# A macaron transformer layer on eight cores: four blocks instead of two transposed by TensorE in the first stage, W1 in two halves, one more first cycle taken into that stage, and statistics from two instructions instead of four

## The chip, the cores and the metric

One Trainium2 chip, eight cores, one sequence (4096 tokens by 1024 features) on each; the cores run the same program and exchange nothing. The metric is the device time of the slowest core in microseconds (us).

## The reference

For each sequence, with `ln` a layer norm without weights:

```
x = x + 0.5 * ffn(ln(x));  x = x + attention(ln(x));  x = x + 0.5 * ffn(ln(x))

ffn(x):  gf = sigmoid(small net of the mean of x over all tokens)
  three times:  tf = sigmoid(gelu(gelu(gelu(out@w1+b1)@w2+b2)@w3+b3)@w4+b4)    # one number a token
                c = 0.1 + adaptive_range * (0.7*gf + 0.3*tf - 0.5) * 2
                out = out + c * [p_r, -p_i, -o_r, o_i]        # quarters o_r o_i p_r p_i of out
```

The attention is causal and linear, with a memory term; it takes no part in the change. The mean over the tokens has to be known before the first coupling `c`, so nothing past the first call of the coupling net can start before every token is normalised.

## The kernel before

The tokens go in 8 blocks of 512, each of 4 tiles of 128. Every engine has its program written out by hand, and the tables at the head of the file set which piece stands where; nothing is moved by a scheduler. There are four stages: P (normalise all tokens), A (first ffn), B (attention), C (second ffn). The change is in P and at the start of A.

**Stage P** runs over the tiles i = 0 to 31. SP's queue loads tile i into a ring of 8 (`x0_ring`), DVE takes its statistics (four `bn_stats` over 256 features and one `bn_aggr`), GpSimd makes scale and bias of a pair of tiles, ACT writes the normalised tile as bf16 (`xtok`, `xtok_b`) three iterations later, TensorE adds the tokens up (`token_sums`, one matmul column for each 128 features and tile). SP waits for the normalised tile i-8 before it loads tile i, since that frees its place in the ring. Blocks 0 and 1 are transposed by TensorE (`transposes`, then copied to `xt` by ACT and DVE). Blocks 2 to 7 are stored to HBM and come back through DMA transposes (`load_xt`), two of which, for blocks 2 and 3, stand in SP's queue ahead of the loads of tiles 24 and 28.

**The UV groups.** W1 is applied once for each block: 24 groups of four matmuls, in threes. K (`xs` times W1, `xs` a sum of features) is copied by ACT to `kt`; U and V are joined with `kt` by DVE to the tiles `u` and `v`. DVE prepares `w1n` and changes two parts of `w1` first (`prepare_w1`), four instructions over 2048 elements.

**A cycle** (block b, k = 0, 1, 2) is the coupling net: ACT makes `h1` by gelu in four parts (`gelu1`), TensorE runs layer 2 (32 matmuls), ACT gelus its four banks (`gelu2`), layer 3 (8 matmuls), `gelu3`, layer 4 (2), `tanh4`. From the tanh DVE makes `c` and the next `p1` (`coupled`), ACT the next `h1`. UV groups of a later block stand as fillers in three places of each cycle: behind layer 2, behind layer 3, behind layer 4 (`FILL`). Cycle 0 of block 0 stands within stage P (`P_L2`, `P_L3`, `P_L4`: the iterations of its layers), since it needs no `c`. In each block of A, ACT also forms the new x of the block before (`spread`, four instructions for each tile), DVE adds it (`combine`), and ACT normalises it for stage B.

**PSUM.** All 8 banks go round in the order in which TensorE takes them (`Banks`): a group waits until the bank taken eight places earlier is read out. K's bank is freed by ACT's copy, U's and V's by DVE.

Of the kernel before, what the change touches and what calls it, by code (L numbers as in the profile page):

```python
# [38 lines left out]
FILL_FIRST = [(0, 0, 0), (2, 2, 5), (2, 3, 0)]  # L39
# [11 lines left out]
P_UV = {**{4 + i: (0, i) for i in range(8)}, **{12 + i: (1, i) for i in range(5)},  # L51
        18: (1, 5), 19: (1, 6), 20: (1, 7), 24: (2, 0), 25: (2, 1)}
P_L2, P_L3, P_L4 = 17, 19, 20
P_SUMS = {4 * b + 7: b for b in range(2, NB - 1)}
P_LAST = 10
# [15 lines left out]

def fillers(ph, b, k, place):
# [3 lines left out]
    if ph == "A" and b == 0:  # L76
        items += [("UV", ahead, g) for g in part(FILL_FIRST, k, place, P_LAST)]
    elif ahead is not None:
        items += [("UV", ahead, g) for g in part(FILL, k, place)]
# [57 lines left out]
def emit(plan, final):  # L137
# [56 lines left out]
    v_x, _ = sb("v_x", [128, DT, T], BF16, xa3 + 8192)  # L194
    gw1c, _ = sb("gw1c", [128, DT, 512], BF16, xa + 16384)
# [62 lines left out]
    bnq, _ = sb("bnq", [128, 2, NTT, 4, 6], F32)  # L258
# [9 lines left out]
    qsum, _ = sb("qsum", [128, NTT, 4], F32)  # L268
# [36 lines left out]
    w1_ld = sig("w1_ld")  # L305
# [46 lines left out]

    def xt_item(ph, b):
        return "ABC".index(ph) * NB + b
# [20 lines left out]
    def tensor_program(te):  # L375
# [21 lines left out]
        def xt_ready(ph, b):  # L397
            if ph == "A" and b < 2:
                te.wait_ge(*freed_at(("T", "P", b, 1)))
                te.wait_ge(*freed_at(("T", "P", b, 3)))  # L400
            else:
                te.wait_ge(*xt_ld[b % 2].at((ph, b)))

        def uv_group(ph, b, g):
# [3 lines left out]
            if g == 0:  # L408
                xt_ready(ph, b)
                te.wait_ge(*xs_ok.at((ph, b)))  # L410
                te.wait_ge(*w1n_ok.at(ph))
            bk = take(("UV", ph, b, g))
            for n in range(4):
                if which == 0:
                    lhs, rhs = w1[:, K_TILES[n], cols], ffn[ph]["xs"][:, n, :]
# [278 lines left out]
    def scalar_program(s):  # L694
        def normalize(ph, b, tt):
# [30 lines left out]
        def transposed(b):  # L726

            for bk2 in range(2):
                bk, use = banks.at(("T", "P", b, bk2))
                s.wait_ge(bank_full[bk], use + 1)  # L730
                s.activation(out=pair(xt[:, b], bk2),
# [58 lines left out]
        def tanh4(ph, b, k):  # L790
            if b > 0 and k == 0:
# [3 lines left out]
            s.activation(out=ffn[ph]["th"][:, k, :], in_=ps[:, bk, :], func=AF.Tanh, scale=0.5,  # L795
# [42 lines left out]
        def cycle(ph, b, k):  # L838
            if k > 0:
# [3 lines left out]
            if b > 0 and k == 1:  # L843
# [3 lines left out]
            if b > 0 and k == 2 and ph == "A":  # L847
                normalize("A", b - 1, 1)
            if ph == "A" and b > 1 and k == 0:
                normalize("A", b - 2, 3)  # L850
            gelu2(ph, b, k)
            filler(ph, b, k, 0)
            if k == 2 and b + 1 < NB:
                for p in range(3):
                    gelu1(ph, b + 1, 0, p)
            gelu3(ph, b, k)
            filler(ph, b, k, 1)
            if k == 2 and b + 1 < NB:
                gelu1(ph, b + 1, 0, 3)
            tanh4(ph, b, k)  # L860
            if b > 0 and k < 2:
                spread(ph, b - 1, 2 * k)
            if b > 0 and k == 2:
# [29 lines left out]
        for i in range(4, 32):  # L893
            if i >= 7:
                normalize("P", (i - 3) // 4, (i - 3) % 4)
            if i == P_L3:
                gelu3("A", 0, 0)
            if i == P_L4:
                s.wait_ge(*misc_ok.at("misc"))
                tanh4("A", 0, 0)  # L900
            if i in P_UV:
                k_group("A", P_UV[i][0], 3 * P_UV[i][1])
            if i == 10:
                transposed(1)
# [12 lines left out]
        for b in range(NB):
            for k in range(3):
                if b > 0 or k > 0:
# [51 lines left out]
    def vector_program(v):  # L971
# [5 lines left out]
        def statistics(ph, b, tt):  # L977
# [10 lines left out]
            for q in range(4):  # L988
                i = v.bn_stats(out=bnq[:, b % 2, tt, q, :], in_=src[:, q * 256:(q + 1) * 256])
# [4 lines left out]
        def transposed(b):  # L994

            for bk2 in range(2, 4):
                bk, use = banks.at(("T", "P", b, bk2))
                v.wait_ge(bank_full[bk], use + 1)
                v.tensor_copy(out=pair(xt[:, b], bk2),
# [20 lines left out]
        def feature_sums(ph, b):  # L1020

            if ph == "A" and b < 2:
# [4 lines left out]
            if b > 0:  # L1027
# [3 lines left out]
            x, xs = xt[:, b % 2], ffn[ph]["xs"]  # L1031
# [4 lines left out]
        def prepare_w1(ph):  # L1036

            w1n = ffn[ph]["w1n"]
            if ph == "C":
                v.wait_ge(*freed_at(("QK", "q", NB - 1, DT - 1)))  # L1040
                v.scalar_tensor_tensor(out=w1n[:, 0:2, :], in0=w1[:, 0:2, :], scalar=2.0,
                                       in1=w1[:, 4:6, :], op0=ALU.mult, op1=ALU.add)
                v.scalar_tensor_tensor(out=w1n[:, 2:4, :], in0=w1[:, 6:8, :], scalar=2.0,
                                       in1=w1[:, 2:4, :], op0=ALU.mult,
                                       op1=ALU.add).then_inc(*w1n_ok.up(ph))
                return
            v.wait_ge(*w1_ld.at("w1"))
# [671 lines left out]
```

## Time and profile before

| what | us |
|---|---|
| median of 3 runs (1725.27 to 1735.0) | 1725.83 |
| the profiled execution, device time | 1724.32 |
| its span, slowest core (6); all cores 1715.6 to 1722.8 | 1722.8 |
| PE busy in the span | 1594.4 (93%) |
| DVE, ACT busy | 1004.0, 894.1 |
| first layer 2 that needs `c` (block 0, cycle 1) starts | 145.74 |
| cycle 0 of block 2 starts | 230.37 |

The span counts from the first to the last instruction of the core. A start time in a row is in us from the span's start.

### The profile page before, as it was taken

What the parts mean: (1) busy time and instruction counts of PE and PEld (TensorE: products, weight loads), DVE (VectorE), ACT (ScalarE), POOL (GpSimd) and SP (SyncE); (2) the same over time, 40 slices, a digit from 0 to 9 for tenths busy, and PEclk for the clock granted to TensorE, in tenths of its full rate; (3) what the DMA queues carried; (4) which work ended last, traced back from release to release, by engine and by line L of the source; (5) the groups of instructions that cost most, each with busy time, mean ns of one, the idle gap of its engine ahead of it and who ended that gap; (6) DMA issues with size and microseconds to landing.
All of it is one profiled execution on the core that took longest, in us unless ns stands there. A gap on an engine that the chain in (4) does not pass through costs nothing.

```text
span 1722.8 us, 27449 instructions; the slowest of 8 cores (1715.6 to 1722.8 us)
## 1 busy us (share of the span) xinstructions
PE 1594.4 (93%) x8166; PEld 726.6 (42%) x8166; DVE 1004.0 (58%) x1856; ACT 894.1 (52%) x1350; POOL 303.6 (18%) x873
## 2 busy tenths in 40 slices
PE   3947999999998999999999999999999999999973
PEld 1423444444443444444444444444444444444431
DVE  4865665565465574536364554545465566767653
ACT  2554787776678714050413233241525677777774
POOL 2541232122023220101101020202020011011111
PEclk9978999999999999999999999999999999999996
DMA  8897124563175983132415142332331123332223
GB/s 196 193 292 163 56 84 124 142 159 105 55 157 131 218 223 90 71 104 68 129 37 159 25 147 50 123 74 86 92 123 25 25 97 101 121 116 81 98 98 122
DMA packets 171422, 196.56 MB, mean 114 GB/s; under 512 B 125328, under 2 KB 132496, under 8 KB 170000
## 3 DMA queue, kind: packets, MB, share of 16 engines
q1 hardware_dynamic: 149024, 111.18, 24.5%
q0 software_dynamic: 22256, 83.64, 16.6%
q8 instruction: 71, 1.16, 0.3%
q14 instruction: 71, 0.58, 0.1%
HBM read 100.16 MB, written 80.74 MB: 105 GB/s over the span
## 4 chain that ended last, share of the span: by engine, by line
PE 83%; ACT 5%; DVE 5%; issue 3%; DMA 2%; SPq 2%; POOL 0%; DVEq 0%; ACTq 0%; POOLq 0%
PE ps L431 20%; PE ps L514 13%; PE ps L420 12%; PE ps L566 7%; PE ps L503 6%; PE ps L579 6%; PE ps L594 6%; PE ps L442 5%; PE ps L489 3%; PE ps L538 2%; PE ps L583 2%; DMA x_ring<-hs 1%; ACT h_a L773 1%; SPq L1598 1%; ACT h_c L773 1%
## 5 line engine op out<-in xcount | busy, mean ns | idle before, releaser
L723 ACT ACTIVATE xtok<-xr,st_nmr,st_r 128x1024 bf16<-128x1024 f32 x32 | 39.7, 1240 | 312.5 <-POOL st_nmr L1408 312.5
L431 PE MATMUL ps<-h_a,w 128*128 128x512 bf16 x768 | 176.0, 387 | 17.6 <-ACT h_a L773 16.8
L431 PE MATMUL ps<-h_c,w 128*128 128x512 bf16 x768 | 175.9, 386 | 16.7 <-ACT h_c L773 16.6
L874 ACT ACTIVATE ebuf<-ps 128x512 bf16<-128x512 f32 x128 | 76.1, 595 | 130.9 <-PE ps L514 127.6
L420 PE MATMUL ps<-xt,w 128*128 128x512 bf16 x512 | 135.0, 387 | 0.0
L431 PEld LDWEIGHTS ps<-h_a,w 128*128 128x128 bf16 x768 | 74.1, 99 | 117.5 <-issue 36.8
L431 PEld LDWEIGHTS ps<-h_c,w 128*128 128x128 bf16 x768 | 73.9, 99 | 117.2 <-issue 37.4
L566 PE MATMUL ps<-wmo,sq 128*128 128x512 bf16 x512 | 121.3, 383 | 1.0 <-DVE xr L1256 1.0
L1364 POOL TENSOR_SCALAR tmp<-mv 128x1 f32<-128x1 f32 (+2 forms) x56 | 13.3, 238 | 602.8 <-DVE mv L991 600.9
L503 PE MATMUL ps<-wvo,xt 128*128 128x512 bf16 x512 | 113.0, 379 | 0.0
L514 PE MATMUL ps<-xt,wk_sb 128*128 128x512 bf16 x512 | 111.8, 379 | 0.0
L514 PE MATMUL ps<-xt,wq_sb 128*128 128x512 bf16 x512 | 111.8, 379 | 0.0
L579 PE MATMUL ps<-s_bf,sq 128*128 128x512 bf16 x448 | 105.8, 379 | 0.0
L1012 DVE SCALAR_TENSOR_TENSOR u_c<-ps,pack,kt_C 128x512 bf16<-128x512 f32 x64 | 47.9, 749 | 94.7 <-ACT kt_C L745 88.2
L594 PE MATMUL ps<-v_sb,skt 128*128 128x512 bf16 x448 | 97.8, 379 | 0.0
L1012 DVE SCALAR_TENSOR_TENSOR u_a<-ps,pack,kt_A 128x512 bf16<-128x512 f32 x56 | 41.8, 747 | 81.7 <-ACT kt_A L745 77.7
L1173 DVE TENSOR_SCALAR ebuf<-ebuf 128x512 bf16<-128x512 bf16 x128 | 37.2, 290 | 82.4 <-ACT ebuf L874 81.6
L780 ACT ACTIVATE h_C<-ps,pack 128x512 bf16<-128x512 f32 x96 | 58.1, 688 | 51.1 <-PE ps L431 51.1
L773 ACT ACTIVATE h_c<-p_c 128x1024 bf16<-128x1024 bf16 x64 | 65.9, 1053 | 31.0 <-DVE p_c L1102 28.4
L420 PE MATMUL ps<-xs_A,w 128*128 128x512 bf16 x256 | 68.3, 391 | 14.2 <-DVE xs_A L1033 7.8
L773 ACT ACTIVATE h_a<-p_a 128x1024 bf16<-128x1024 bf16 x64 | 65.9, 1053 | 29.4 <-DVE p_a L1102 26.3
L1261 DVE SCALAR_TENSOR_TENSOR xr<-ps,rlm,xr 128x512 f32<-128x512 f32 x64 | 48.0, 750 | 54.2 <-PE ps L583 50.3
(217 smaller groups left out, 2891.5 us busy)
## 6 DMA issues: line engine op xcount, KB each, us to landing
x_d<-xr POOLq DMA_DIRECT2D x64, 512.0 KB, 3.7
xr<-x_d SPq DMA_DIRECT2D x60, 512.0 KB, 3.6
x_ring<-hs SPq DMA_DIRECT2D x32, 512.0 KB, 8.4
xr<-hs SPq DMA_DIRECT2D x32, 512.0 KB, 4.5
xn_d<-xtok POOLq DMA_DIRECT2D x64, 256.0 KB, 3.2
out<-xr POOLq DMA_DIRECT2D x32, 512.0 KB, 3.1
sk_d<-sk SPq DMA_DIRECT2D x7, 1024.0 KB, 5.1
w<-cw POOLq DMA_DIRECT2D x6, 512.0 KB, 14.5
```

Source lines behind the costliest of these rows:

```text
L420: i = te.matmul(out=ps[:, bk, :], lhsT=lhs, rhs=rhs, start=(n == 0), stop=(n == 3))
L431: i = te.matmul(out=ps[:, bks[et], :], lhsT=w2[:, kt, et * 128:(et + 1) * 128], rhs=ffn[ph]["h1"][:, kt, :], start=(kt == 0), stop=(kt == ...
L442: i = te.matmul(out=ps[:, bks[et], :], lhsT=w3[:, kt, et * 128:(et + 1) * 128], rhs=ffn[ph]["h2"][:, kt, :], start=(kt == 0), stop=(kt == 3))
L503: i = te.matmul(out=ps[:, bk, :], lhsT=xt[:, b % 2, dt, tt * 128:(tt + 1) * 128], rhs=wvo[:, dt, eh * T:(eh + 1) * T], start=(dt == 0), st ...
L514: i = te.matmul(out=ps[:, bk, :], lhsT=w_sb[:, dt, et * 128:(et + 1) * 128], rhs=xt[:, b % 2, dt, :], start=(dt == 0), stop=(dt == DT - 1))
L566: i = te.matmul(out=ps[:, bk, :], lhsT=sq[:, dt, tt * 128:(tt + 1) * 128], rhs=wmo[:, dt, eh * T:(eh + 1) * T], start=(dt == 0), stop=(dt ...
L579: te.matmul(out=ps[:, bk, :], lhsT=sq[:, dt, tt * 128:(tt + 1) * 128], rhs=s_bf[:, dt, eh * T:(eh + 1) * T], start=(dt == 0), stop=False)
L594: i = te.matmul(out=ps[:, bk, :], lhsT=skt[:, jt, dt * 128:(dt + 1) * 128], rhs=v_sb[:, jt, eh * T:(eh + 1) * T], start=(jt == 0), stop=(j ...
L773: s.activation(out=pair(ffn[ph]["h1"], p), in_=src, func=AF.Gelu).then_inc(*h1_ok.up((ph, b, k, p)))
L780: s.activation(out=ffn[ph]["h2"][:, et, :], in_=ps[:, bk, :], func=AF.Gelu, bias=pack[:, P_B2 + et:P_B2 + et + 1]).then_inc(bank_free[bk], 1)
L874: s.activation(out=ebuf[:, n % 2, :], in_=ps[:, bk, :], func=AF.Exp).then_inc(*e_ok.up(n))
L1012: v.scalar_tensor_tensor(out=u[:, et, :], in0=ps[:, bk, :], scalar=pack[:, P_B1 + et:P_B1 + et + 1], in1=ffn[ph]["kt"][:, et % 2, :], op0= ...
```

## The change

- **Four blocks are transposed by TensorE** (`P_TURNED`, `P_T`: blocks 1, 2, 3 at i = 10, 15, 22). Blocks 0 to 3 are neither stored nor loaded back, and the two DMA transposes leave SP's queue in stage P.
- **W1 comes in two column halves**, eight loads instead of four. `prepare_w1` runs for each half (the second at i = 6). SP no longer waits for W1 before it loads tile 4. The loads of W2 and W3 are issued by GpSimd behind tile pair 4 instead of 2, those of the small net behind pair 9 instead of 6.
- **Cycle 0 of block 1 moves into stage P** (layers at i = 24, 26, 27), with its own buffers `th_1` and `xs_1`. Four thirds of block 2's UV groups stand in P instead of two, so 12 groups; with the four at the end 16 of 24. Block 1 has two cycles in stage A, which hold all 24 groups of block 3 and the spreads and normalised tiles of block 0. DVE does block 1's first `coupled` and `turn` at the end of block 0's last cycle.
- **Statistics** are two `bn_stats` over 512 elements. Their input alternates between two quarters of the features, 1024 bytes apart, so that the even and the odd half of the result are a quarter each, and GpSimd needs one instruction less for a block. This holds for stage B's statistics too.
- The load of `wv` for stage B is issued after block 1's couplings instead of after the small net.

```diff
-FILL_FIRST = [(0, 0, 0), (2, 2, 5), (2, 3, 0)]
+FILL_FIRST = [(0, 0, 3), (1, 1, 3), (0, 0, 0)]
+FILL_SECOND = [(0, 0, 0), (4, 4, 6), (5, 5, 0)]
...
+P_TURNED = 4
+P_T = {10: 1, 15: 2, 22: 3}
+P_L2 = {17: 0, 24: 1}
...
 def xt_ready(ph, b):
-            if ph == "A" and b < 2:
+            if ph == "A" and b < P_TURNED:
...
         def cycle(ph, b, k):
-            if k > 0:
+            second = (ph, b) == ("A", 1)
+            if k > first_cycle(ph, b):
                 for p in range(4):
                     gelu1(ph, b, k, p)
                 filler(ph, b, k - 1, 2)
...
             tanh4(ph, b, k)
-            if b > 0 and k < 2:
+            if second:
+                spread(ph, 0, 2 * k - 2)
+                spread(ph, 0, 2 * k - 1)
+                if k == 2:
+                    normalize("A", 0, 1)
+            elif b > 0 and k < 2:
                 spread(ph, b - 1, 2 * k)
...
         def statistics(ph, b, tt):
-            for q in range(4):
-                i = v.bn_stats(out=bnq[:, b % 2, tt, q, :], in_=src[:, q * 256:(q + 1) * 256])
+            for q in range(2):
+                i = v.bn_stats(out=bnq[:, b % 2, tt, q, :],
+                               in_=src[:, q * 512:(q + 1) * 512].rearrange("p (c j) -> p j c", c=2))
...
+        def prepare_w1(half_):
+            w1n = ffn["A"]["w1n"][:, :, half_ * 512:(half_ + 1) * 512]
+            w = w1[:, :, half_ * 512:(half_ + 1) * 512]
+            v.wait_ge(*w1_ld[half_].at("w1"))
...
         for i in range(SEQ // 128):
-            if i == 4:
-                q.wait_ge(*w1_ld.at("w1"))
-            if i == 24:
-                load_xt("A", 2)
-            if i == 28:
-                load_xt("A", 3)
...
-            if i >= 16:
+            if i - 8 >= 4 * P_TURNED:
                 store_normalized(i - 8)
```

The order on TensorE in stage P from i = 23 to i = 27, before (L525 token sums, L420 the UV groups of i = 24 and 25; nothing stands at i = 22 and 26):

```order
L525 MATMUL ps<-onesz,xtok 128x1 x32
L420 MATMUL ps<-xs_A,w_43 128x512 x4
L420 MATMUL ps<-xt,w_43 128x512 x4
L420 MATMUL ps<-xt,w1n_A 128x512 x4
L420 MATMUL ps<-xs_A,w_43 128x512 x4
L420 MATMUL ps<-xt,w_43 128x512 x4
L420 MATMUL ps<-xt,w1n_A 128x512 x4
L525 MATMUL ps<-onesz,xtok_b 128x1 x32
```

And now, from i = 22 to 26 (L415 transposes, L448 UV groups, L553 token sums, L459 layer 2, L470 layer 3):

```order
L415 MATMUL ps<-idb,xtok_b 128x128 x32
L553 MATMUL ps<-onesz,xtok_b 128x1 x32
L448 MATMUL ps<-xs_A,w_43 128x512 x4
L448 MATMUL ps<-xt,w_43 128x512 x4
L448 MATMUL ps<-xt,w1n_A 128x512 x4
L553 MATMUL ps<-onesz,xtok 128x1 x32
L459 MATMUL ps<-h_a,w_44 128x512 x32
L448 MATMUL ps<-xs_A,w_43 128x512 x4
L448 MATMUL ps<-xt,w_43 128x512 x4
L448 MATMUL ps<-xt,w1n_A 128x512 x4
L470 MATMUL ps<-h_A,w_45 128x512 x8
```

Block 3's transposes and a second layer 2, with its layer 3, have come in between the UV groups.

TensorE in cycle 2 of block 0, with the layer 2 that starts it and the one behind it, before:

```order
L431 MATMUL ps<-h_a,w_44 128x512 x32
L420 MATMUL ps<-xt,w_43 128x512 x4
L420 MATMUL ps<-xt,w1n_A 128x512 x4
L442 MATMUL ps<-h_A,w_45 128x512 x8
L420 MATMUL ps<-xs_A,w_43 128x512 x4
L420 MATMUL ps<-xt,w_43 128x512 x4
L420 MATMUL ps<-xt,w1n_A 128x512 x4
L451 MATMUL ps<-h_A,w4r 128x512 x2
L431 MATMUL ps<-h_a,w_44 128x512 x32
```

And now, with the last three groups of cycle 1 ahead (L459, L470, L479 are layers 2, 3 and 4):

```order
L448 MATMUL ps<-xs_A,w_43 128x512 x4
L448 MATMUL ps<-xt,w_43 128x512 x4
L448 MATMUL ps<-xt,w1n_A 128x512 x4
L459 MATMUL ps<-h_a,w_44 128x512 x32
L470 MATMUL ps<-h_A,w_45 128x512 x8
L479 MATMUL ps<-h_A,w4r 128x512 x2
L459 MATMUL ps<-h_a,w_44 128x512 x32
```

Between layers 2, 3 and 4 of block 0's cycle 2 nothing stands any more.

ACT in block 1 from the tanh of cycle 1 to the `gelu2` of cycle 2, before (L759 spread, L773 `gelu1`, L745 the copy of K, L723 normalise):

```order
L795 ACTIVATE th_A<-ps,misc 128x512
L759 ACTIVATE tq_a<-xr,tk 128x256 x4
L773 ACTIVATE h_a<-p_a 128x1024 x4
L745 ACTIVATE kt_A<-ps 128x512
L723 ACTIVATE xtok<-xr,tk 128x1024
L780 ACTIVATE h_A<-ps,pack 128x512 x4
```

And now, the same place (L790 spread, L804 `gelu1`, L776 the copy of K, L752 normalise):

```order
L826 ACTIVATE th_A<-ps,misc 128x512
L790 ACTIVATE tq_a<-xr,tk 128x256 x8
L804 ACTIVATE h_a<-p_a 128x1024 x4
L776 ACTIVATE kt_A<-ps 128x512 x2
L752 ACTIVATE xtok<-xr,tk 128x1024
L811 ACTIVATE h_A<-ps,pack 128x512 x4
```

Two spreads stand ahead of the four parts of `gelu1`, and the copies of K behind them.

## Rows read from the trace of the kernel before

**Rows 1.** Busy time by stretch: us, engines, then clock, DMA share, GB/s.

```profile
40.00:60.00 20.00, 20.00 (x146) 10.53 (x145) 19.07 (x47) 11.91 (x15) 8.98 (x26) 1.00 0.63 117
...
100.00:120.00 20.00, 8.77 (x59) 4.06 (x59) 13.51 (x38) 10.09 (x10) 10.10 (x29) 0.71 0.99 274
120.00:140.00 20.00, 8.64 (x116) 5.05 (x117) 7.68 (x25) 6.89 (x12) 8.76 (x30) 0.52 0.70 242
```

**Rows 2.** Chain that ended last, two issues in it: start, us, what.

```profile
90.12 8.52 SPq L1598
...
104.32 9.62 SPq L1598
```

**Rows 3.** Waits of SP's queue, 0 to 60 us: total, times, longest.

```profile
SPq L1622 <- DMA w<-cw: 20.9, 1, 20.9
```

**Rows 4.** Timeline of DVE, first stage: start, length, instruction, idle before.

```profile
29.98 1.22 DVE L1048 TENSOR_TENSOR w1n_A<-w 128x2048 bf16<-128x2048 bf16 x1
...
43.85 1.40 DVE L989 BATCH_NORM_STATS2 bnq<-x_ring 128x6 f32<-128x256 f32 x4
...
45.53 0.74 DVE L1012 SCALAR_TENSOR_TENSOR u_a<-ps,pack,kt_A 128x512 bf16<-128x512 f32 x1
...
46.79 1.40 DVE L989 BATCH_NORM_STATS2 bnq<-x_ring 128x6 f32<-128x256 f32 x4
...
58.52 1.28 DVE L999 COPY xt<-ps 128x1024 bf16<-128x1024 bf16 x2
...
89.33 0.75 DVE L1012 SCALAR_TENSOR_TENSOR u_a<-ps,pack,kt_A 128x512 bf16<-128x512 f32 x1 [5.81 <-ACT kt_A L745]
...
127.62 0.26 DVE L991 BATCH_NORM_AGGREGATE mv<-bnq 128x2 f32<-128x24 f32 x1
```

**Rows 5.** Timeline of PE, first stage and blocks 0 and 1.

```profile
78.61 7.07 PE L431 MATMUL ps<-h_a,w 128*128 128x512 bf16 x32
...
145.74 8.81 PE L431 MATMUL ps<-h_a,w 128*128 128x512 bf16 x32 [5.22 <-ACT h_a L773]
...
178.58 7.07 PE L431 MATMUL ps<-h_a,w 128*128 128x512 bf16 x32
185.49 1.03 PE L420 MATMUL ps<-xs_A,w 128*128 128x512 bf16 x4
...
187.21 1.89 PE L442 MATMUL ps<-h_A,w 128*128 128x512 bf16 x8
188.94 1.03 PE L420 MATMUL ps<-xt,w1n_A 128*128 128x512 bf16 x4
...
190.67 0.59 PE L451 MATMUL ps<-h_A,w4r 128*128 128x512 bf16 x2
191.10 1.03 PE L420 MATMUL ps<-xt,w 128*128 128x512 bf16 x4
...
230.37 7.07 PE L431 MATMUL ps<-h_a,w 128*128 128x512 bf16 x32 [0.17 <-issue]
```

**Rows 6.** Timeline of ACT, the same stretch.

```profile
85.13 2.42 ACT L780 ACTIVATE h_A<-ps,pack 128x512 bf16<-128x512 f32 x4 [5.85 <-PE ps L431]
...
88.55 0.61 ACT L745 ACTIVATE kt_A<-ps 128x512 f32<-128x512 f32 x1
...
130.24 2.37 ACT L723 ACTIVATE xtok_b<-x_ring,st_nmr,st_r 128x1024 bf16<-128x1024 f32 x2 [2.50 <-POOL st_nmr L1377]
...
173.77 2.96 ACT L773 ACTIVATE h_a<-u_a 128x1024 bf16<-128x1024 bf16 x3
...
191.99 2.06 ACT L759 ACTIVATE tq_a<-xr,tk 128x256 f32<-128x256 f32 x4
```

**Rows 7.** DVE's groups by line and shape, whole span: count, busy, mean ns.

```profile
L1080 DVE STREAM_TRANSPOSE ctr_A<-th_A 32x384 f32<-32x384 f32 x32 | 18.2, 569 | 13.2 <-ACT th_A L795 12.8
...
L1217 DVE TENSOR_TENSOR a_t<-ps,mask 128x512 bf16<-128x512 f32 x8 | 5.5, 692 | 21.8 <-PE ps L538 21.8
...
L1217 DVE TENSOR_TENSOR a_t<-ps,mask 128x256 bf16<-128x256 f32 x8 | 3.4, 424 | 2.2 <-PE ps L538 2.2
```

More of the change, by code:

```diff
@@ L76, in fillers @@
     if ph == "A" and b == 0:
-        items += [("UV", ahead, g) for g in part(FILL_FIRST, k, place, P_LAST)]
+        items += [("UV", ahead, g) for g in part(FILL_FIRST, k, place, P_LAST + 4)]
+    elif ph == "A" and b == 1:
+        items += [("UV", ahead, g) for g in part(FILL_SECOND, k, place)]
     elif ahead is not None:
@@ L304, in emit @@
     skt_ld = sig("skt_ld")
-    w1_ld = sig("w1_ld")
+    w1_ld = [sig(f"w1_ld{i}") for i in range(2)]
     w2_ld = sig("w2_ld")
@@ L842, in cycle @@
                 filler(ph, b, k - 1, 2)
-            if b > 0 and k == 1:
+            if b > 0 and k == 1 and not second:
                 spread(ph, b - 1, 1)
@@ L1077, in token_couplings @@
                 v.wait_ge(*tok_ok.at((ph, b - 1)))
-            rows = ffn[ph]["th"][:, :, :].rearrange("p k t -> p (k t)")
-            for q in range(4):
-                i = v.transpose(out=ffn[ph]["ctr"][32 * q:32 * q + 32, :, :],
-                                in_=rows[32 * q:32 * q + 32, :].rearrange(
-                                    "p (a t) -> p a t", t=128)[:, :, 32 * q:32 * q + 32])
+            k0 = first_cycle(ph, b)
+            parts = [(ffn[ph]["th"][:, k0:, :].rearrange("p k t -> p (k t)"), 4 * k0, 12)]
+            if k0 == 1:
+                parts.append((tanh_row(ph, b, 0), 0, 4))
+            for rows, first, last in parts:
+                for q in range(4):
+                    i = v.transpose(out=ffn[ph]["ctr"][32 * q:32 * q + 32, first:last, :],
+                                    in_=rows[32 * q:32 * q + 32, :].rearrange(
+                                        "p (a t) -> p a t", t=128)[:, :, 32 * q:32 * q + 32])
             i.then_inc(*ctr_ok.up((ph, b)))
@@ L1221, in attention @@
             if b == NB - 1:
[L1222 removed]
+                restore_w1n()
             bk, use = banks.at(("D", b))
@@ L1301, in vector_program @@
         feature_sums("A", 0)
-        prepare_w1("A")
+        prepare_w1(0)
         token_sums("P", 0)
@@ L1489, in gpsimd_program @@
         step(g.memset(half[:, 0:1], -0.5))
-        step(g.memset(tmp[:, :, :], 0.0))
-        g.memset(qsum[:, :, :], 0.0).then_inc(*iota_ok.up("iota"))
-        load(w1, cw1, DT, 2, w1_ld, "w1")
+        g.memset(tmp[:, :, :], 0.0).then_inc(*iota_ok.up("iota"))
+        g.wait_ge(*iota_ok.at("iota"))
+        for h in range(2):
+            c = slice(512 * h, 512 * (h + 1))
+            load(w1[:, :, c], cw1[:, :, c], DT, 2, w1_ld[h], "w1")
         for j in range(2 * NB):
```

203 lines of the change are left out of this document (117 added, 86 removed).

## The prediction

> **What bounds the kernel now.** I read the windows first, then the chain that ended last, then SP's waits, then the three timelines. PE is the bound of the whole, but not of stage P: in 100 to 140 us it is busy 17.4 of 40 us, at a granted clock of 0.71 and 0.52 [rows 1]. In 40 to 60 us DVE is busy 19.07 of 20 us [rows 1]: an iteration takes 43.85 to 46.79 = 2.94 us, of which the statistics are 1.68 (to the next instruction at 45.53) and the U and V of one third 1.26 [rows 4]. Two things break that pace. At the layer 2 of i = 17 DVE waits 5.81 us for `kt` [rows 4], because ACT's copy stands behind the four parts of `gelu2` and a normalise [rows 6]: from the start of layer 2 (78.61) to the U behind it (89.33) it is 10.7 us [rows 4, 5]. And in the chain stand the two DMA transposes, which hold SP's queue for 8.52 and 9.62 us [rows 2], so that the last tiles are asked for late. Before that SP had waited 20.9 us for W1 [rows 3].
>
> The stage ends when the last tile is normalised, 130.24 + 2.37 = 132.6 [rows 6]; the first layer 2 that needs `c` starts 13.1 us later, at 145.74, and block 2's first cycle at 230.37 [rows 5]. From there on the two programs do the same work, so the question is how far that point moves.
>
> **Stage P, before its first layer 2.** The four parts of `prepare_w1` at 2048 elements take 1.22 us each, from 29.98 on [rows 4]; a half takes four of about 0.6, and one wait, so 32.6 in place of 34.7. PE can do its first K meanwhile, and the first iteration ends at about 36.8. The statistics: the row of 512 elements against that of 256 gives 692 - 424 = 268 ns for 256 elements [rows 7], so of the 350 ns for one `bn_stats` about 70 are fixed; two of 512 take 1.2 to 1.27 us instead of 1.40, which leaves 1.55 for a tile and 2.80 for an iteration. So i = 6 starts at 39.6 (before 43.85). Then DVE pays 2.5 for the second half of W1, 1.3 for each transposed block (58.52 starts such a copy, 1.28 [rows 4]) and the sums of features as before: i = 10 ends at 56.1, i = 12 at 65.7 (PE's wait for `xs` as before), i = 15 at 74.1. PE then transposes block 2 and sums it, and layer 2 starts at 75.7 instead of 78.61.
>
> **From there to the end of stage P.** With 10.7 us from layer 2 to the next U, and 2.8 for each further iteration that has U and V, i = 18 ends at 87.7, i = 21 at 97.0, i = 23 (with block 3's transposes in between) at 102.8. The second layer 2 starts at about 101 (behind the third at i = 23 and its token sums), so U of i = 25 comes at 111.8, and DVE waits nearly 6 us again, a stall that was not there. i = 26, 27, 28 end at 116.0, 117.5 and 120.3, and three statistics later DVE is through at 125.0 (before 127.62 + 0.26 = 127.9 [rows 4]). The way from there to the normalised tile was 4.7 us (GpSimd's four instructions and ACT's two), so the stage ends at 129.7 instead of 132.6. Removing the two transposes from SP takes 18.1 us out of the chain and brings only 2.9: what is late next is DVE, held by ACT and PE at two layers 2. The loads are early enough: tile 31 can be asked for at 113, when tile 23 is normalised, and is wanted at 123.4. Two more short stretches of transposes and token sums may leave the clock low at a layer 2; I take 0.9 us for that. **Stage P: -2.0 us.** The 13.1 us behind it stay, since three groups are now done in a gap of 5.22 us on PE [rows 5].
>
> **From the first layer 2 to block 2.** Before, 230.37 - 145.74 = 84.6 us. In them lie five cycles and 38 groups. A cycle's own layers are 6.91 + 1.73 + 0.43 = 9.07 us (178.58 to 185.49, 187.21 to 188.94, 190.67 to 191.10), two groups 1.73 [rows 5]: 45.4 + 32.8 = 78.2, so 6.4 us are idle or slow. Now four cycles and 29 groups: 36.3 + 25.1 = 61.3. What is added by waits:
> - 1.7 us as before for the low clock at the first layer 2 (8.81 for 7.07 [rows 5]).
> - Block 0, cycle 1: one group behind layer 2 and one behind layer 3, for gelus of 2.42 and 1.26 us, and three behind layer 4, 2.6 us, for a way through tanh, `c`, `p1` and gelu of 4.7 us: 2.9 us.
> - Block 0, cycle 2: no group at all. Behind layer 2 ACT does `gelu2` (2.42 [rows 6]), then three parts of block 1's `gelu1` (2.96 [rows 6]), then `gelu3` (1.2). Layer 4 ends about 7.2 us behind layer 2, and PE works 2.2 of them: 5.0 us.
> - Block 1, cycle 1 to 2: ACT does two spreads (2 x 2.06 [rows 6]) ahead of the four parts of `gelu1`, and only then copies K. The fourth bank that the next layer 2 takes is that of such a K group (eight takes earlier), so it waits for tanh 0.74, spreads 4.1, gelus 4.2, copy 0.5 = 9.6 us, under which lie six groups, 5.2 us: 4.4 us.
> - The end of block 1 with two more spreads and three normalised tiles ahead of the next `gelu2`: 1.0, and 1.5 in cycle 0 of block 2, which is past the point and counts all the same.
>
> Together 16.5, so 77.8 instead of 84.6: **-6.8 us.** Bounds: if none of the new waits appears (they are worked out, not seen) it is -17; if the clock falls to the lower level in the two long ones it is some 3 us less, so -4.
>
> Edits that I cost at nothing: the later load of `wv`, since block 3's folds use it a block of some 48 us later; W2, asked for at 54 instead of 45 and wanted at 75.7, which is close, and costs one us for each us it lands later; stage B's statistics, since PE is the bound there; GpSimd's missing instructions.
>
> **Sum.** -2.0 - 6.8 = -8.8 on the profiled execution's 1724.3 (1.5 above its span) gives 1715.5; the median of the runs is 1.5 above that execution, so **1717 us**.
>
> **Rivals.**
>
> *Slower: the interleaved reads cost DVE double.* No row shows DVE reading float32 from SBUF in jumps at each element. The nearest is the 32x384 transpose, which jumps after each 32 elements and takes 569 ns, as 384 elements at 1.05 ns and a fixed part would [rows 7]; by it I take no penalty. At two element times a tile would cost 2.55 instead of 1.55. Stage P is DVE's up to layer 2: the twelve statistics ahead of it (and the work between, unchanged) put it at 87.3, behind it the two waits for `kt` hide a part, and the end comes at 145.7 + 4.7 = 150.4, 17.8 late. With -6.8 it is +11, so 1737. It decides from 0.45 us more for a tile on. The Trainium skill (Advanced Engine Details and Errata, SBUF Cachelines) states that SBUF has 16-byte cachelines, that two hits on a line are needed to absorb the access latency, and that a different line at each access is penalised; the changed input hits a line once. No row here can confirm it, and by that rule this rival is the forecast.
>
> *Faster: stage P runs at DVE's own work.* If the second stall doesn't appear and the first is shorter, DVE needs 32.7 + 28 x 1.55 + 20 x 1.26 + 10 of copies, sums and W1 = 111 for its last tile, 17 earlier than 127.9. With the rest as above it would be -24. Against it stands the row of 5.81 us, for it the loads, which come much earlier. Half of it is likelier than all: 1700 to 1706.
>
> *No change.* Tiles 4 to 7 are now asked for beside W1, and W1 in pieces of half the length. If tile 3 or W1's first half lands 4 us later, or W2 after 75.7, the -2.0 turns into +2, and with the low clock in both new waits 1724 remains. SP might also be held by something other than the transposes; then its gain is nothing, which is the same case.
>
> **Chances.** Forecast 0.45 (own range 1708 to 1725), slower rival 0.27 (1729 to 1746), faster rival 0.15, no change 0.13. The range from 1701 to 1740 leaves out about 2 in 10. Over 1% (17.3 us, about what this kernel's measurement can tell) faster is most of the faster rival and a tail of the forecast: 0.18. Slower by as much is the upper part of the slower rival: 0.09. Within 1%: 0.73.
>
> **What would show it.** One `bn_stats` of 512 at 0.6 to 0.7 us (right) or 1.1 to 1.2 (slower rival). No DMA transpose on SP before 140 us. The two layers 2 of stage P at about 76 and 101, each with DVE waiting some 5 us for `kt`. The last tile normalised near 130. Gaps on PE of 5 us in block 0's cycle 2 and 4 us ahead of block 1's second layer 2, the latter ended by ACT's copy of K. I am wrong where stage P ends much earlier than 125, or if these gaps are filled.

## The result, and the profile after

The changed kernel takes 1736.76 us (median of 12 executions), the kernel before 1726.14 beside it: a ratio of 1.0047, 95% interval [1.0024, 1.0069]. So it is slower, by some 8 to 11 us, where 8.8 us less were predicted. Times of single kernels below are medians over executions whose eight cores lie within 14 us of each other, with their number in brackets; on the same footing this one gives 1736.7 (10).

The start is where to look first. The windows of the changed kernel, its slowest core (columns as in [rows 1]):

```profile
0.00:20.00 20.00, 0.55 (x2) 0.50 (x2) 8.54 (x28) 1.49 (x2) 3.19 (x12) 1.00 0.88 209
20.00:40.00 20.00, 0.00 (x0) 0.00 (x0) 0.00 (x0) 0.79 (x1) 5.53 (x11) 1.00 0.67 106
40.00:60.00 20.00, 13.47 (x92) 7.66 (x94) 10.87 (x19) 6.98 (x8) 5.14 (x17) 0.83 0.38 107
60.00:80.00 20.00, 18.00 (x131) 9.31 (x131) 19.28 (x37) 12.18 (x14) 7.74 (x23) 1.00 0.42 117
```

From 20 to 40 us PE and DVE do nothing at all, and the last row looks like the stretch from 40 to 60 us in [rows 1]: the same stage, 20 us later. The timeline of GpSimd says why:

```profile
2.52 2.36 POOL L1544 DMA_DIRECT2D w<-cw  x3 [0.67 <-POOL tmp L1553]
24.42 2.17 POOL L1544 DMA_DIRECT2D w<-cw  x3 [19.54 <-issue]
31.07 0.72 POOL L1544 DMA_DIRECT2D w<-cw  x1 [4.49 <-issue]
36.45 0.72 POOL L1544 DMA_DIRECT2D w<-cw  x1 [4.65 <-issue]
37.25 0.22 POOL L1427 TENSOR_SCALAR tmp<-mv 128x2 f32<-128x2 f32 x1
```

GpSimd issues three of W1's eight loads, stands for 19.5 us, issues three, and stands twice more. Only then comes the first instruction for the statistics of tiles 0 and 1, which DVE had by 10.7 us (tile 3's by 16.0):

```profile
6.97 1.30 DVE L1029 BATCH_NORM_STATS2 bnq<-x_ring 128x6 f32<-128x512 f32 x2 [0.49 <-DMA x_ring<-hs]
...
15.81 0.21 DVE L1032 BATCH_NORM_AGGREGATE mv<-bnq 128x2 f32<-128x12 f32 x1
46.49 0.69 DVE L1042 COPY xt<-ps 128x1024 bf16<-128x1024 bf16 x1 [30.48 <-PE ps L415]
```

ACT waits for scale and bias just as long, and PE for ACT; the first rows of ACT's and of PE's timeline:

```profile
39.21 4.63 ACT L752 ACTIVATE xtok<-x_ring,st_nmr,st_r 128x1024 bf16<-128x1024 f32 x4 [36.08 <-POOL st_nmr L1440]
```

```profile
49.90 0.81 PE L448 MATMUL ps<-xs_A,w 128*128 128x512 bf16 x3 [1.87 <-DVE xs_A L1078]
```

"issue" as a releaser means that the trace shows nothing that GpSimd waited for. Behind the start the stage runs nearly as worked out, but 20 us late. PE's layers 2 in stage P and behind it, in the changed kernel (answering to [rows 5]):

```profile
96.19 6.85 PE L459 MATMUL ps<-h_a,w 128*128 128x512 bf16 x31 [0.35 <-issue]
...
121.64 7.07 PE L459 MATMUL ps<-h_a,w 128*128 128x512 bf16 x31
...
164.03 7.20 PE L459 MATMUL ps<-h_a,w 128*128 128x512 bf16 x32 [2.60 <-ACT h_a L804]
180.24 8.75 PE L459 MATMUL ps<-h_a,w 128*128 128x512 bf16 x31 [2.14 <-ACT h_a L804]
195.70 7.93 PE L459 MATMUL ps<-h_a,w 128*128 128x512 bf16 x31
221.97 8.45 PE L459 MATMUL ps<-h_a,w 128*128 128x512 bf16 x31 [4.09 <-ACT kt_A L776]
241.05 7.07 PE L459 MATMUL ps<-h_a,w 128*128 128x512 bf16 x32
```

Block 2's first cycle starts at 241.05 against 230.37 before [rows 5], 10.7 us later, which is the whole of the loss. The stretch from the first `c` layer 2 to it is 77.0 us against 84.6.

### The profile page after: what moved, and what is told of

Same layout as the page of the kernel before. It is cut to its first block, busy times and chain, and to the rows that moved or that the text cites. A ratio compares the mean times of both kernels' runs of the same rounds, so it can differ in the third digit from the quotient of the medians.

```text
span 1733.6 us, 27281 instructions; the slowest of 8 cores (1727.2 to 1733.6 us)
## 1 busy us (share of the span) xinstructions
PE 1587.5 (92%) x8072; PEld 729.7 (42%) x8230; DVE 1000.5 (58%) x1740; ACT 896.9 (52%) x1354; POOL 304.3 (18%) x868
## 4 chain that ended last, share of the span: by engine, by line
PE 81%; issue 6%; ACT 5%; DVE 5%; POOL 1%; DVEq 0%; ACTq 0%; POOLq 0%
PE ps L459 20%; PE ps L542 13%; PE ps L448 11%; PE ps L594 6%; PE ps L531 6%; PE ps L622 6%; PE ps L607 6%; PE ps L470 5%; PE ps L517 3%; PE ps L566 2%; PE ps L611 2%; ACT h_a L804 1%; ACT h_c L804 1%; PE ps L479 1%; DVE p_c L1155 1%
## 5 line engine op out<-in xcount | busy, mean ns | idle before, releaser
L752 ACT ACTIVATE xtok<-xr,st_nmr,st_r 128x1024 bf16<-128x1024 f32 x32 | 39.7, 1240 | 309.1 <-POOL st_nmr L1471 309.1
L459 PE MATMUL ps<-h_a,w 128*128 128x512 bf16 x752 | 175.1, 388 | 21.1 <-ACT h_a L804 14.9
L459 PE MATMUL ps<-h_c,w 128*128 128x512 bf16 x752 | 174.7, 386 | 17.9 <-ACT h_c L804 17.0
L448 PE MATMUL ps<-xt,w 128*128 128x512 bf16 x497 | 132.9, 385 | 2.3 <-DVE w L1090 1.5
L459 PEld LDWEIGHTS ps<-h_a,w 128*128 128x128 bf16 x768 | 74.5, 99 | 119.7 <-issue 38.8
L459 PEld LDWEIGHTS ps<-h_c,w 128*128 128x128 bf16 x768 | 73.9, 99 | 117.3 <-issue 37.6
L804 ACT ACTIVATE h_c<-p_c 128x1024 bf16<-128x1024 bf16 x64 | 65.9, 1053 | 31.5 <-DVE p_c L1155 29.0
L804 ACT ACTIVATE h_a<-p_a 128x1024 bf16<-128x1024 bf16 x64 | 65.6, 1054 | 25.9 <-DVE p_a L1155 23.1
L448 PEld LDWEIGHTS ps<-xt,w 128*128 128x128 bf16 x512 | 50.5, 99 | 64.1 <-issue 5.9
```

The source lines that it names most:

```text
L448: i = te.matmul(out=ps[:, bk, :], lhsT=lhs, rhs=rhs, start=(n == 0), stop=(n == 3))
L459: i = te.matmul(out=ps[:, bks[et], :], lhsT=w2[:, kt, et * 128:(et + 1) * 128], rhs=ffn[ph]["h1"][:, kt, :], start=(kt == 0), stop=(kt == ...
L804: s.activation(out=pair(ffn[ph]["h1"], p), in_=src, func=AF.Gelu).then_inc(*h1_ok.up((ph, b, k, p)))
```

## The experiments

**Theory 1:** GpSimd is held while it issues W1 in halves, since the room for its outstanding packets is full. A packet is a piece of a transfer as the profile counts it, and it is outstanding from its issue until it has landed. W1's eight half-width loads have 272 packets each (2176 in all in the trace of the changed kernel), the four whole ones before 144 each. Rivals: W1 lands late beside the tiles (theory 2), or the new order of stage P costs what the start hides (theory 3).

### W1 whole again

```diff
-    w1_ld = [sig(f"w1_ld{i}") for i in range(2)]
+    w1_ld = [sig("w1_ld")] * 2
...
-        for h in range(2):
-            c = slice(512 * h, 512 * (h + 1))
-            load(w1[:, :, c], cw1[:, :, c], DT, 2, w1_ld[h], "w1")
+        load(w1, cw1, DT, 2, w1_ld[0], "w1")
```

> The changed kernel with W1 loaded in four whole pieces again (512 KB each, as in the kernel before); every other part of the change stays, and both half preparations on VectorE wait for the whole of W1. Theory 1 (GpSimd is held while it issues the eight half-width loads, 272 packets each, because three of them, 816 packets, fill the room for outstanding packets and the fourth waits until some have landed; the statistics of the first two pairs stand behind it in GpSimd's program): no idle time between the four loads, the first pair statistics at about 10 us in place of 37.3, the last of VectorE's tile statistics at 125 to 129 us in place of 145.4, and 1714 to 1722 us in all. Theory 2 (the whole of W1 now reads beside the tiles 4 to 7, and what is late is its landing, not its issue): the pair statistics come early but the first K group still starts at about 45 us or later, and the time stays at 1730 to 1736. Theory 3 (the slower time comes from stage P's second first cycle or from the eighth K group, and the start only shifts slack): 1733 to 1737 with an early start.

Measured: 1718.8 us (7), ratio to before 0.9985 [0.9949, 1.0021]. GpSimd's timeline in it:

```profile
2.51 2.31 POOL L1544 DMA_DIRECT2D w<-cw  x4 [0.66 <-POOL tmp L1553]
10.58 0.23 POOL L1427 TENSOR_SCALAR tmp<-mv 128x2 f32<-128x2 f32 x1 [5.76 <-DVE mv L1032]
```

No hold, the pair statistics at 10.58, the first K group on PE at 30.25, 19.6 us earlier than with the halves; the time is 17.9 us less. This one edit undoes the loss; theories 2 and 3 are out, since everything else of the change is still in.

### The halves alone, in the kernel before

```diff
-        load(w1, cw1, DT, 2, w1_ld, "w1")
+        for h in range(2):
+            c = slice(512 * h, 512 * (h + 1))
+            load(w1[:, :, c], cw1[:, :, c], DT, 2, w1_ld, "w1")
```

> The kernel before with one part of the change alone: W1's load in two column halves of four pieces each, eight loads of 256 KB; all else is as before, and everything that needs W1 still waits for both halves. Theory 1 (GpSimd held in its issue): GpSimd idles after the third load, the statistics of pair 0 start behind the last load, at 25 to 38 us in place of 10.9, the first four normalized tiles come 5 to 16 us later than before, and the whole takes 5 to 16 us more: 1731 to 1742. It may be less than in the changed kernel, since here SyncE holds tile 4 back until W1 has landed, so that the loads drain with less beside them. Theories 2 and 3 (landing beside the tiles, or stage P's order): the start is unchanged, since tile 4 still waits: 1725 to 1728.

Measured: 1735.3 us (7), ratio 1.0082 [1.0048, 1.0116].

```profile
2.55 2.36 POOL L1481 DMA_DIRECT2D w<-cw  x3 [0.47 <-issue]
17.39 2.16 POOL L1481 DMA_DIRECT2D w<-cw  x3 [12.49 <-issue]
27.10 1.44 POOL L1481 DMA_DIRECT2D w<-cw  x2 [7.54 <-issue]
28.62 0.22 POOL L1364 TENSOR_SCALAR tmp<-mv 128x2 f32<-128x2 f32 x1
```

The same three loads and the same stop, in a kernel that has nothing else of the change. It is shorter (12.5 us), as expected where SyncE holds back tile 4. PE's first K group comes at 45.83 instead of 34.94, 10.9 us later, and the kernel is 10.8 us slower than before (1724.5 in this group). So here a shift of the start passes to the end one for one.

### More room for descriptors

```diff
-                   dynamic_dma_scratch_size=1024)
+                   dynamic_dma_scratch_size=1728)
...
-    top = [1152]
+    top = [1856]
-    idb, _ = sb("idb", [128, 128], BF16)
+    idb, _ = sb("idb", [128, 128], BF16, r0 + 31872)
```

> The changed kernel with more room in SBUF for the descriptors of GpSimd's loads: 1,728 bytes a partition in place of 1,024 (the tensors above move up, and the identity matrix takes a free place). Theory 1: the held load comes later in the row. The room of 1,024 bytes took 816 packets and not 1088; 1.69 times as much takes 1377 to 1836, so five or six of the eight loads are issued one behind the other (three in the changed kernel), and then the same hold sets in until about 24 us; the two or three that are left keep the pair statistics back until 25 to 33 us, and the time is 1722 to 1735. Rival (the hold comes from other traffic, or from a limit on the number of loads, not from this room): the hold sets in behind the third load again, and the time is 1735 to 1737.

Measured: 1727.8 us (7), ratio 1.0010 [0.9964, 1.0056].

```profile
2.51 4.51 POOL L1544 DMA_DIRECT2D w<-cw  x6 [0.66 <-POOL tmp L1553]
26.62 1.44 POOL L1544 DMA_DIRECT2D w<-cw  x2 [19.61 <-issue]
```

Six loads instead of three go without a stop, in the same order beside the same tile loads; the room is what holds GpSimd, and the number of loads is not.

### Whole rows in eight loads

```diff
-        for h in range(2): ...
+        load(w1, cw1, DT, 1, w1_ld[0], "w1")
```

> The changed kernel with W1 loaded in eight pieces of one whole row tile each (256 KB, 144 packets if a whole row is one packet per partition as in the kernel before), in place of eight half-width pieces of 272 packets; room for descriptors 1,024 bytes as in both kernels. The three rooms tried so far took 816 packets and not 1088 (1,024 bytes), 1088 and not 1360 (1,152), 1632 and not 1904 (1,728). Theory 1a, room in packets, one a byte of that setting: seven of these loads (1008 packets) go one behind the other, the eighth (1152) is held until the first have landed; pair 0's statistics start behind it, somewhere in 12 to 25 us. Rival 1b, room in loads or in bytes moved: the hold comes behind the third load, as it does with the half-width pieces of the same size in KB, and pair 0's statistics start at 30 us or later, 1730 to 1737 us. Rival 1c, room without a sharp edge: no hold, pair 0 at 10.6 us, 1715 to 1720 us.

Measured: one execution of 1728.7 us. W1 is now 1152 packets in eight loads of 256 KB, and seven of them go:

```profile
2.50 3.97 POOL L1544 DMA_DIRECT2D w<-cw  x7 [0.66 <-POOL tmp L1553]
31.01 0.55 POOL L1544 DMA_DIRECT2D w<-cw  x1 [24.54 <-issue]
```

Loads of the same size in KB as the halves, but seven for three: the limit is in packets. Seven are 1008 and pass at 1,024 bytes, four half loads are 1088 and do not. From an empty start the room takes one packet for each byte of the setting, as far as the steps tell: 1088 pass at 1,152, 1632 pass and 1904 don't at 1,728. The hold of a single small load lasts 24.5 us, so it is no matter of the held load's own size. Pair 0's statistics start behind it at about 31.6 us, later than the 12 to 25 that were expected of theory 1a.

The packets' own times say more of when room comes free. The DMA view up to 30.3 us has 1007 of GpSimd's packets, so all but one of the seven loads' 1008 had begun, and the eighth is issued at 31.01. In the changed kernel all 816 of the first three loads stand in the view up to 23.7 us, and the fourth is issued at 24.42. By one packet a byte there would have been room for the held load as soon as 128 and 64 packets had landed, long before. So at 1,024 bytes the first hold ends only when everything issued is through. It is not always so: at 1,728 bytes the seventh load is issued at 26.62, when 1363 of 1632 packets have begun. By what rule room comes free stays open; a count of free packets alone it isn't.

### The first half, the statistics, then the second half

```diff
-        for h in range(2): ...
+        load(w1[:, :, 0:512], cw1[:, :, 0:512], DT, 2, w1_ld[0], "w1")
         for j in range(2 * NB):
             pair_statistics(j)
+            if j == 1:
+                load(w1[:, :, 512:1024], cw1[:, :, 512:1024], DT, 2, w1_ld[1], "w1")
```

with 1,152 bytes of room.

> The changed kernel with W1 still in halves, but the second half's four loads are issued behind the statistics of the first block's two pairs, and the room for descriptors is 1,152 bytes a partition in place of 1,024. Theory 1 with room in proportion: the first half's four loads are 1088 packets and the room takes 918 to 1224, so they go without a hold if it is above 967 packets at 1,024 bytes; the pair statistics then start at 9 to 10 us and 15 to 16 us, the second half is issued at about 18 to 30 us, the first K group starts by about 35 us, and the time is 1712 to 1720. If the fourth load is held, pair 0 waits for it until about 24 us and the time is 1722 to 1728. Theory 3 (stage P's order or the eighth K group are to blame): 1733 to 1737 whatever the start does.

Measured: 1718.2 us (4), ratio 0.9981 [0.9925, 1.0038]. The first half's four loads go without a stop, the pair statistics start at 10.16 and 14.84, and all of block 0 is transposed by 22.5, some 5 us before the kernel with W1 whole. It gains nothing, since PE then waits for the half of W1:

```profile
22.32 1.04 PE L553 MATMUL ps<-onesz,xtok 128*128 128x1 bf16 x32
29.44 1.87 PE L448 MATMUL ps<-xs_A,w 128*128 128x512 bf16 x4 [6.08 <-DMA w<-cw]
```

That is 0.8 us earlier than with W1 whole (30.25), although only half of it is asked for. So the point of the halves, to have the first columns early, does not come about: with the tiles beside it the first half isn't there before 29 us. The DMA queues up to 29 us (packets, MB, share of the 16 engines; q0 has GpSimd's loads, q1 SP's) show what goes instead, first with W1 whole, then with the half:

```profile
q0 software_dynamic: 576, 2.10, 47.1%
q1 hardware_dynamic: 1181, 3.82, 44.2%
```

```profile
q1 hardware_dynamic: 1762, 5.94, 65.5%
q0 software_dynamic: 1088, 1.05, 29.1%
```

In the same time GpSimd's queue brings half the bytes in nearly twice the packets, and the tile loads bring 5.94 MB in place of 3.82. And the hold has only moved: the second half's loads meet the first's.

```profile
29.66 2.99 POOL L1544 DMA_DIRECT2D w<-cw  x4 [13.00 <-issue]
```

GpSimd stands for 13.0 us again, until the 1088 packets of the first half are through.

### VectorE's halves together

On top of W1 whole:

```diff
         prepare_w1(0)
+        prepare_w1(1)
...
             if i == 6:
-                prepare_w1(1)
+                pass
```

> The kernel with W1 whole and, in addition, both of VectorE's half preparations at one place, behind the first block's feature sums, as in the kernel before. The work is the same; the first groups' U and V wait 2.6 us longer. If the halves of the preparation gain what the prediction put on them (2.7 us at the start, given back where VectorE is the bound of that stage): the first U group 2.6 us later, the last tile statistics 0 to 1 us later, 1718 to 1721 us. If the end of the stage follows its start: 2 to 3 us slower, 1720 to 1723.

Measured: 1714.8 us (2), ratio 0.9896 [0.9808, 0.9984], beside 1718.9 (6) of its partner, the kernel with W1 whole, without this edit; the median core is at 1709.4 against 1711.0. The first U group comes 2.7 us later, as expected (36.75 against 34.05 on core 0), but the last tile statistics don't: they end at 121.4 to 123.9 us on the eight cores, against 122.3 to 126.3 and 123.4 to 126.2 in the two traces of the partner. Neither expectation has that: what the two halves of the preparation win at the start does not reach the end of the stage, and put together they end it rather earlier. Why wasn't tried, and that the whole kernel is faster than its partner two executions don't show.

### The bank of block 1's second layer 2

On top of W1 whole:

```diff
-FILL_SECOND = [(0, 0, 0), (4, 4, 6), (5, 5, 0)]
+FILL_SECOND = [(0, 0, 0), (4, 4, 5), (6, 5, 0)]
```

> The changed kernel with W1 loaded whole, and the second block's fillers (4, 4, 5), (6, 5, 0) in place of (4, 4, 6), (5, 5, 0): one U group moves from behind the second cycle's fourth layer to the cycle's last place, so that the fourth PSUM bank that block 1's next layer 2 takes comes from a group that VectorE frees and not from a K group that ScalarE frees late. The wait of TensorE for that K group measured 4.09 us before block 1's second layer 2 both in the changed kernel and with W1 whole. If the bank is the whole wait: it falls to below 1 us and the fastest and the mean core gain 3 to 4 us, 1713 to 1716 us for the slowest core. Rival (ScalarE's queue is late there for whatever comes, h_a included): another wait of 2 to 4 us takes its place and the time is 1718 to 1720.

Measured: 1715.1 us (4), ratio 0.9946 [0.9889, 1.0003]. PE's row there:

```profile
198.00 7.07 PE L459 MATMUL ps<-h_a,w 128*128 128x512 bf16 x32 [1.49 <-ACT h_a L804]
```

The wait is 1.49 us for `h_a` in place of 4.09 for `kt`. From the first `c` layer 2 to this one it is 54.4 us on core 0, with W1 whole alone 58.1. Both theories hold a part: the bank was the larger wait, and ScalarE's gelu stands 1.5 us behind it. But the median core gains only 1.0 us, so it was run once more beside its partner, the kernel with W1 whole.

> The kernel with W1 whole and the moved bank once more, now beside the kernel with W1 whole alone. In the first run of it the wait before block 1's second layer 2 fell from 4.09 to 1.49 us (for h_a), the start of block 2's second cycle came 3.6 us earlier on core 0, and yet its spans (1708.1 to 1713.5 us) are no shorter than those of the kernel with W1 whole (1708.2 to 1717.4). Between 520 and 560 us its granted clock was 0.91 and 0.91 where core 0 of the other had 1.00. Theory A (the clock gives it back there, on each core on which the earlier work leaves TensorE idle in that place): the median core is 0 to 1.5 us faster than the kernel with W1 whole, and 470 to 700 us is at a mean clock of 0.97 on most cores. Theory B (the two runs' spread hid it): 3 to 4 us faster on the median core, 1713 to 1716 us for the slowest.

> The changed kernel with W1 loaded whole once more, as the partner of the two others in this group. It gave 1719.15 us with a ratio of 0.9985, its cores 1708 to 1718 us; the kernel before gave 1716 to 1725 on its cores. Expected again: 1717 to 1720 us, the median core at 1711 to 1712 and 8 us below the kernel before, of which the slowest core shows 5 to 6.

Measured: 1715.1 us (3), ratio 0.9899 [0.9812, 0.9986], and for the partner 1718.9 (6), ratio 0.9940 [0.9902, 0.9979]; the median core is at 1710.8 and 1711.0. So the slowest core gains 3.8 us and the median core nothing, although block 2's first cycle starts at 214.3 to 218.7 us on the eight cores, against 217.8 to 223.3 without the moved bank. Where it goes shows in the windows of core 0, first W1 whole (its first run), then with the moved bank (its second):

```profile
520.00:540.00 20.00, 16.00 (x72) 6.96 (x72) 12.91 (x21) 17.33 (x29) 8.90 (x19) 1.00 0.60 124
540.00:560.00 20.00, 17.65 (x82) 8.07 (x84) 10.17 (x16) 14.81 (x22) 2.79 (x5) 1.00 1.12 171
```

```profile
520.00:540.00 20.00, 16.65 (x65) 6.95 (x64) 11.46 (x18) 14.58 (x23) 8.40 (x16) 0.83 0.60 123
540.00:560.00 20.00, 16.83 (x72) 7.24 (x72) 8.43 (x13) 14.34 (x22) 1.62 (x3) 0.91 1.10 215
```

The granted clock falls there in the second and not in the first, by 0.17 and 0.09 of 20 us each, which is up to 5 us of work at the full clock; over 470 to 700 us the mean is 0.96 or 0.97 on seven of eight cores with the moved bank (six in its first run), and 0.99 on six of eight without. Theory A's place and size hold; that the earlier arrival is what brings the fall is argued from these runs, and why it would wasn't tried.

### Groups moved out of the first stage

```diff
-        ... 26: (2, 2), 28: (2, 3)}
+        ... 26: (2, 2)}
-P_LAST = 12
+P_LAST = 9
-FILL_FIRST = [(0, 0, 3), (1, 1, 3), (0, 0, 0)]
+FILL_FIRST = [(0, 0, 3), (1, 2, 3), (1, 1, 0)]
```

> The kernel with W1 whole and the moved bank, and in addition block 2's groups 9 to 11, now in the last part of the first stage, move into the first cycles behind it (three groups more in the fillers of block 0). VectorE is the engine that ends that stage: its last tile statistics lie behind the U and V work of these groups, 1.43 us. Expected: the last statistics 1.2 to 1.5 us earlier; of the added 2.6 us of TensorE in the cycles 1.6 us fall into waits for ScalarE (2.1 and 2.8 us in block 0's cycles) and 1 us adds; 0 to 1 us faster than the kernel with the bank moved alone. Rival (the cycles have no slack because what follows the fillers is queued behind them): 1 to 2 us slower than it.

Measured: 1719.4 us (2), the median core 1715.7 against 1709.8 with the bank alone: slower. The last statistics do come earlier, starting at 122.79 instead of 124.96 on core 0, but PE's wait ahead of layer 4 in block 0's last cycle grows from 2.82 to 7.60 us:

```profile
177.75 1.16 PE L479 MATMUL ps<-h_A,w4r 128*128 128x512 bf16 x2 [7.60 <-ACT h_A L818]
```

and VectorE's timeline shows what is late ahead of it:

```profile
167.66 0.75 DVE L1055 SCALAR_TENSOR_TENSOR u_x<-ps,pack,kt_A 128x512 bf16<-128x512 f32 x1 [5.20 <-PE ps L448]
170.26 0.69 DVE L1060 TENSOR_TENSOR v_x<-kt_A,ps 128x512 bf16<-128x512 f32 x1 [1.86 <-PE ps L448]
170.87 0.54 DVE L1144 TENSOR_SCALAR cbf_A<-th,misc 128x512 bf16<-128x512 f32 x1
```

VectorE's U and V of the added fillers stand in its program ahead of block 1's `c`, and wait for PE groups that now lie behind layers 2 and 3. `c`, `p1` and ScalarE's gelus come some 4 us later (`c` at 170.87 for 166.26). The rival is right, at more than twice its price. The empty places in block 0's last cycle are not slack: VectorE's products for the next block lie under them.

### The interleaved statistics alone, in the kernel before

```diff
-            for q in range(4): ... in_=src[:, q * 256:(q + 1) * 256]
+            for q in range(2): ... in_=src[:, q * 512:(q + 1) * 512].rearrange("p (c j) -> p j c", c=2)
```

> The kernel before with the interleaved statistics alone: two instructions over 512 elements that alternate between two quarters, in place of four over 256, and GpSimd's sums read them so; nothing else is changed. The prediction took 1.2 to 1.27 us a tile against 1.40, and its slower rival 2 us or more. In the trace of the changed kernel the pair takes 1.29 us and the aggregation 0.21 against 0.26. Expected: 0.15 us a tile less on VectorE and 1724 to 1727 us in all, no change that can be measured, since SyncE's late tiles set the end of that stage (tiles waited for at 115.8 to 124.3 us). If the interleaved reads cost time elsewhere (GpSimd's or ScalarE's work beside them): 1728 or more.

Measured: one execution of 1722.9 us beside 1724.0 (7); ratio 1.0012 [0.9956, 1.0069], no change. VectorE's group in the first stage:

```profile
L989 DVE BATCH_NORM_STATS2 bnq<-x_ring 128x6 f32<-128x512 f32 x64 | 41.4, 689 | 12.0 <-DMA x_ring<-hs 11.5 <-issue 0.2 <-DVE misc L1296 0.2
```

689 ns for 512 alternating elements, where 256 in a row cost 411 in the kernel before. No run has these statistics over 512 in a row; the nearest is another operation of VectorE over 512 float32 elements in a row, 692 ns [rows 7]. So there is no penalty to be seen, and double time, 1.1 to 1.2 us, is out.

## Why the prediction was wrong

**The term that failed is the start of stage P.** The prediction costed W1's halves only as VectorE's preparation ("a half takes four of about 0.6") and as a landing that might be late; "If tile 3 or W1's first half lands 4 us later" was the rival. It put the issue at nothing, without a reason: twice as many loads of half the row stand in GpSimd's program ahead of the pair statistics, and no term or rival reads GpSimd's timeline there. Measured: a hold of 19.5 us and two of some 4.6, which moves i = 6 to 60.00 instead of the predicted 39.6. The halves alone cost 10.8 us in the kernel before and 17.9 in the changed one.

**With that term taken out the rest can be compared.** Predicted, and measured with W1 whole (core 7, the slowest):

| point | predicted | W1 whole | changed kernel |
|---|---|---|---|
| statistics of i = 6 start | 39.6 | 40.42 | 60.00 |
| first, second layer 2 of stage P | 75.7, 101 | 76.50, 102.01 | 96.19, 121.64 |
| DVE's waits for `kt` behind them | 5.8, nearly 6 | 4.33, 4.77 | 4.39, 5.09 |
| last tile statistics end | 125.0 | 125.93 | 145.56 |
| last tile normalised | 129.7 | 131.60 | 151.26 |
| first layer 2 with `c` | 142.8 | 144.36 | 164.03 |
| from there to block 2 | 77.8 | 79.0; core 0 77.3 | 77.0 |
| time | 1717 | 1718.8 | 1736.7 |

- *DVE is late next once the two transposes leave SP:* right. With W1 whole SP issues no DMA transpose before 140 us. In the changed kernel it issues nothing but tile loads from 1.5 to 79 us, 18 in one row:

```profile
1.52 77.27 SPq L1689 DMA_DIRECT2D x_ring<-hs  x18
```

  and with W1 whole DVE is through within 1 us of the forecast.
- *The second stall, at the layer 2 of i = 24, was not there before:* right, 5 us. The faster rival falls with it.
- *-6.8 us behind stage P:* measured 77.0 to 79.0 against 84.6, so -5.6 to -7.6. Of the waits the one for K's bank was sized 4.4 and is 4.09. The long one in block 0's cycle 2 was sized 5.0 and is 0.28 + 2.82, with 1.7 of slower clock in layer 2 (8.75 for 7.07). That the sum is met this closely is partly luck, as the layers 2 of W1 whole show on core 7:

```profile
144.36 7.20 PE L459 MATMUL ps<-h_a,w 128*128 128x512 bf16 x32 [2.60 <-ACT h_a L804]
160.57 8.75 PE L459 MATMUL ps<-h_a,w 128*128 128x512 bf16 x32 [2.14 <-ACT h_a L804]
176.03 9.60 PE L459 MATMUL ps<-h_a,w 128*128 128x512 bf16 x32
203.96 8.75 PE L459 MATMUL ps<-h_a,w 128*128 128x512 bf16 x32 [4.09 <-ACT kt_A L776]
223.34 7.07 PE L459 MATMUL ps<-h_a,w 128*128 128x512 bf16 x32
```

  The prediction had 1.7 us of low clock, at the first of them, where it is 0.1. The three behind it take 5.9 us more than 7.07 each, and waits that were sized too long make up for most of it.
- *The slower rival's time, 1737, is the measured one by chance; its mechanism is false.* One `bn_stats` of 512 takes 0.69 us. The Trainium skill (Advanced Engine Details and Errata, SBUF Cachelines) says that a different cacheline at each access is penalised. The measurement does not bear that out for this access: alternation between two places 1024 bytes apart shows no penalty in either kernel.
- *The median:* with W1 whole the median core is 9.6 us below the kernel before (1710.8 against 1720.4 us), the slowest core only 5.7. Two of its eight cores had a granted clock of 0.91 over the first 200 us and the others 0.92 to 0.95, and these two end at 1716 and 1717 where the others are at 1708 to 1712. They are also the only ones at 0.97 over 470 to 700 us, the others being at 0.99. In its second trace it is again the two cores at 0.97 there that end at 1717, though one of them had 0.93 over the first 200 us and a core with 0.92 ended at 1712. So the later stretch marks the slow cores better than the first. The metric takes the slowest, so an uneven clock took back 4 us of the gain.

The best version that ran more than twice has W1 whole and the moved bank: 1715.1 us in both groups, where the kernel before gave 1724.0 and 1724.8.

## What to carry to other kernels

Cut into columns, W1's loads kept their bytes and had nearly four times the packets in all (2176 for 576), and the engine that issues them was held in its own program. Count the outstanding packets against the room, and look at what stands behind the issue on that engine, not only at who waits for the data. An idle stretch whose releaser is "issue", between loads of one engine, is the sign. And a first part that is asked for alone need not come early: here half of W1, in 1088 packets beside the tile loads, was there at about 29 us, when the whole in 576 packets was.

## What the runs showed of the hardware

- GpSimd's loads are held by a room for packets: 1008 outstanding pass and 1088 do not at 1,024 bytes of descriptor space a partition, 1088 pass at 1,152, and 1632 but not 1904 at 1,728. A held load of 144 packets stood for 24.5 us, until the 1008 ahead of it were through; a hold behind 816 packets ended likewise, one at 1,728 bytes with some 270 packets still to begin. The Trainium skill (DMA: Bandwidth & Descriptors, SWDGE vs HWDGE vs iDMA) says that GpSimd appends descriptors to rings in SBUF from which the DMA engines drain them. No trace here shows a ring, but the holds, which move with the size of that space, fit one that fills up and stops GpSimd.
- Beside tile loads, 576 packets with 2.10 MB and 1088 packets with 1.05 MB both took until about 29 us.
- An issue on GpSimd costs about 0.72 us at 272 packets (2.17 for three) and about 0.58 at 144 (2.31 for four).
- Statistics over 512 float32 elements that alternate between two places 1024 bytes apart take 0.69 us, as another VectorE operation over 512 in a row does.
- Behind a gain of 3.6 us at 200 us the granted clock was lower at 520 to 560 us (0.83 to 0.92 for 1.00 on most cores), and the median core ended no earlier. That the one brings the other is not shown.
